# Transposed score pairs six slots behind the score pairs instead of five, and one DMA per half of the row maxima, in a fused ViT tower block

## The reference

```python
gray  = einsum('bchw,c->bhw', x, (0.2989, 0.587, 0.114))
edges = conv3x3(gray, scharr)                       # two filters
h     = (|edges[0]| + |edges[1]|) / 2               # 256 rows of 256: the tokens
h     = concat([cls_tok, h], axis=1)                # 257 tokens of width 256
y     = layernorm(h)
q, k, v = split(y @ w_qkv + b_qkv)                  # 16 heads of 16
att   = softmax(where(causal, q k^T / 4, -inf))     # 257 x 257, per head
h     = h + (att v) @ w_out + b_out
xq    = fake_quant(layernorm(h))                    # one scale for the whole tensor
u     = fake_quant(silu(xq @ wq_gate^T) * (xq @ wq_up^T))
out   = h + u @ wq_down^T
```

## Time and profile before

| | us |
|---|---|
| median of three runs | 1346.86 (1345.83 to 1353.33) |
| the profiled execution, its own time | 1357.62 |
| span of the profiled execution, first to last instruction | 1355.9 |
| PE busy, in the span | 1036.2 (76%) |
| DVE / ACT / POOL busy | 857.1 / 685.5 / 537.8 |
| mean granted TensorE clock | 0.881 of full speed |

### The profile page before, as it was taken

The page is one execution under the profiler, slowest core; times in us unless marked ns, Lnnn a source line. Parts: engine busy times, 40 slices in busy tenths (PEclk is TensorE's granted clock), DMA queues, the critical chain, the costliest instruction groups (busy, mean ns, idle before and its releaser), DMA issues. The chain is left out here.

```text
span 1355.9 us, 28643 instructions
## 1 busy us (share of the span) xinstructions
PE 1036.2 (76%) x9565; PEld 711.0 (52%) x9574; DVE 857.1 (63%) x1987; ACT 685.5 (51%) x1171; POOL 537.8 (40%) x645
## 2 busy tenths in 40 slices
PE   2458888888898988988898898887743766636665
PEld 1236666666666666666666666666532333313332
DVE  2134656667666676666676755664555888888664
ACT  1235555556555555655565555544223676633332
POOL 4244554465555555555555554543210000003222
PEclk9978989899999899999999988987766999976656
DMA  3565445555455554554565544423200334401764
GB/s 102 142 136 143 109 113 126 131 128 150 111 141 132 131 131 124 150 136 127 126 147 130 135 120 109 106 61 101 68 10 1 128 138 160 170 1 48 234 233 160
DMA packets 158498, 164.38 MB, mean 121 GB/s; under 512 B 29384, under 2 KB 153196, under 8 KB 155372
## 3 DMA queue, kind: packets, MB, share of 16 engines
q1 hardware_dynamic: 158444, 163.68, 44.4%
HBM read 73.26 MB, written 34.12 MB: 79 GB/s over the span
## 5 line engine op out<-in xcount | busy, mean ns | idle before, releaser
L519 ACT ACTIVATE prob<-ST 128x772 f32<-128x772 f32 x256 | 209.6, 819 | 218.3 <-PE ST L929 215.1
L684 DVE TENSOR_REDUCE mneg<-SX 128x2 f32<-128x258 f32 x256 | 107.6, 420 | 313.6 <-PE SX L915 313.1
L912 PE MATMUL SX<-kst,qst 96*128 96x257 bf16 (+1 forms) x1024 | 168.7, 259 | 44.1 <-DMA qst<-qpart 39.4
L929 PE MATMUL ST<-qst,kst 98*128 98x256 bf16 (+2 forms) x1536 | 145.5, 229 | 45.5 <-DMA qst<-mpart 45.0
L686 DVE TENSOR_REDUCE mneg<-SX 128x2 f32<-128x514 f32 x256 | 173.9, 679 | 0.0
L929 PEld LDWEIGHTS ST<-qst,kst 98*128 98x128 bf16 x1536 | 124.6, 102 | 69.3 <-DMA qst<-mpart 32.8
L915 PE MATMUL SX<-mask_s,ident_b 128*128 128x256 bf16 x512 | 148.2, 290 | 0.0
L912 PEld LDWEIGHTS SX<-kst,qst 96*128 96x128 bf16 x1024 | 97.1, 102 | 90.0 <-issue 64.3
L445 POOL TENSOR_SCALAR_AFFINE_SELECT prob<-prob 128x1016 f32<-128x1016 f32 x128 | 142.3, 1112 | 0.0
L1512 PE MATMUL GU<-qst,hq 128*128 128x256 bf16 (+1 forms) x384 | 87.2, 379 | 49.1 <-ACT hq L1303 49.1
L948 PE MATMUL G<-prob,vaug 128*32 128x256 f32 (+2 forms) x3072 | 118.9, 285 | 2.6 <-POOL prob L445 2.5
(11 more groups left out here) (228 smaller groups left out, 2106.0 us busy)
## 6 DMA issues: line engine op xcount, KB each, us to landing
kst<-kpart SPq DMA_DIRECT2D x192, 128.5 KB, 2.5
gst<-gray_dram SPq DMA_DIRECT2D x96, 256.0 KB
qst<-qpart SPq DMA_DIRECT2D x192, 128.0 KB, 2.4
h_dram<-hb SPq DMA_DIRECT2D x12, 1280.0 KB, 4.6
hb<-h_dram SPq DMA_DIRECT2D x12, 1280.0 KB, 6.1
wg_raw<-in_x SPq DMA_DIRECT2D x48, 256.0 KB, 4.0
wu_raw<-in_x SPq DMA_DIRECT2D x48, 256.0 KB, 4.1
gray_dram<-gray SPq DMA_DIRECT2D x64, 128.0 KB, 2.8
```

What stands on the lines that cost most here:

```text
L519: nc.scalar.activation(prob[:, g % 2, 2 * (u % 2):2 * (u % 2) + 2, 0:QEND], ST[:, :, 0:QEND], ACT.Exp).then_inc(exp_done, 1)
L684: nc.vector.tensor_reduce(mneg[:, 0, u // 4, 0, at], SX[:, :, S0:S0 + P + 1], AX.X, ALU.max, negate=True)
L912: mm(SX[:, r, at:at + k], qst[par][0:SR, 2 * u + r, P * t:P * t + P], kst[par][0:SR, 2 * u + r, 0:k], start=t == 1, stop=False)
L929: last = mm(ST[0:KEYS[k], r, QAT[k]:QAT[k] + QN[k]], kst[par_][:, i, KFIRST[k]:KFIRST[k] + KEYS[k]], qst[par_][:, i, Q0[k]:IMG], start=Tru ...
```

## The change

Four things are changed, all in the first stage.

1. The transposed pairs move one slot later: slot u now has `scores_t` of pair u+2 of `bT` (slots 0 to 5) and of pair u-6 of `bS` (slots 6 and 7); before, it was pair u+3 (slots 0 to 4) and pair u-5 (slots 5 to 7). ACT's exponentials move with them.
2. The PV quads move one slot later: quad 0 from slot 7 to slot 0 of the next step, quads 1, 2 and 3 from slots 1, 3 and 5 to slots 2, 4 and 6. POOL's `select` of quad 0 moves behind the two additions of the gray image.
3. `max_rows` sends both extra rows of a half (top and low part of the maxima) in one DMA instead of two.
4. DVE's `split(bS, 0)` is done before `edge_stats(bC)` instead of after it.

```diff
@@ sync: max_rows
                     wait(sp, msplit, b, 2, half_ + 1)
-                    for i in range(2):
-                        sp.dma_start(qst[par][SR + i:SR + i + 1, 8 * half_:8 * half_ + 8, :],
-                                     mpart[half_][8 * i:8 * i + 8, :]).then_inc(m_loaded[half_], 16)
+                    sp.dma_start(qst[par][SR:SR + 2, 8 * half_:8 * half_ + 8, :], mpart[half_][:, :]
+                                 ).then_inc(m_loaded[half_], 16)
@@ gpsimd: step
-                select(bS, 0)
                 if valid(bO):
...
                     nc.gpsimd.tensor_tensor(gray[:, :, :], gray[:, :, :], src(2), ALU.add).then_inc(gray_step, 1)
+                select(bS, 0)
@@ scalar: step
-                exponential(bT, 3)
+                exponential(bT, 2)
                 absolute(0)
                 keys(0)
+                exponential(bT, 3)
+                keys(1)
                 exponential(bT, 4)
-                keys(1)
-                exponential(bT, 5)
                 queries(0)
                 absolute(1)
-                exponential(bT, 6)
+                exponential(bT, 5)
...
                 unnormalised(0)
-                exponential(bT, 7)
+                exponential(bT, 6)
...
-                exponential(bS, 0)
+                exponential(bT, 7)
...
+                exponential(bS, 0)
                 unnormalised(1)
-                exponential(bS, 1)
...
-                exponential(bS, 2)
+                exponential(bS, 1)
@@ vector: step
                 edge_tile(bC, 1)
+                split(bS, 0)
                 edge_stats(bC)
-                split(bS, 0)
@@ tensor: step
                 scores(0)
-                scores_t(bT, odd, 3)
+                scores_t(bT, odd, 2)
                 edges(0)
                 keys(0)
+                outputs(bT, odd, 0)
                 scores(1)
+                scores_t(bT, odd, 3)
+                keys(1)
+                scores(2)
                 scores_t(bT, odd, 4)
                 outputs(bT, odd, 1)
-                keys(1)
-                scores(2)
-                scores_t(bT, odd, 5)
                 spread_rec()
                 queries(0)
                 edges(1)
                 scores(3)
-                scores_t(bT, odd, 6)
-                outputs(bT, odd, 2)
+                scores_t(bT, odd, 5)
                 queries(1)
                 turn_max(0)
                 scores(4)
-                scores_t(bT, odd, 7)
+                scores_t(bT, odd, 6)
+                outputs(bT, odd, 2)
...
                 project(0)
                 project(1)
                 scores(5)
+                scores_t(bT, odd, 7)
+                scores(6)
                 scores_t(bS, par, 0)
                 outputs(bT, odd, 3)
-                scores(6)
-                scores_t(bS, par, 1)
                 values()
                 transposes()
                 scores(7)
-                scores_t(bS, par, 2)
-                outputs(bS, par, 0)
+                scores_t(bS, par, 1)
                 turn_max(1)
```

More of the change, by code:

```diff
@@ L699, in split @@
                     wait(dve, mT_done, b, 2, half_ + 1)
-                    wait(dve, m_loaded[half_], b - 1, 32, 32)
+                    wait(dve, m_loaded[half_], b - 1, 16, 16)
                     nc.vector.tensor_copy(mpart[half_][:, :], M[1][0:H, 0:IMG]).then_inc(msplit, 1)
@@ L924, in scores_t @@
                         if u % 4 == 0:
-                            wait(pe, m_loaded[u // 4], b, 32, 32)
+                            wait(pe, m_loaded[u // 4], b, 16, 16)
                         for r in range(2):
```

## The result

| | before | changed |
|---|---|---|
| median of four runs, us | 1346.34 (1341.0 to 1353.33) | 1425.86 (1423.16 to 1429.68) |
| ratio, 95% interval | 1 | 1.0589 (1.0533 to 1.0646) |
| profiled execution, own time / span, us | 1357.62 / 1355.9 | 1423.16 / 1421.4 |
| mean granted clock in the span | 0.881 | 0.879 |
| mean step well inside the loop (19 periods of the keys' starts), us | 27.39 | 30.30 (28.7 to 32.2) |

The changed kernel is slower by 5.9%. The sum had 1423 us for the profiled execution, and that came to 1423.16. Against the median the forecast of 1412 is 14 us low: the profiled execution before lay 10.8 us over its median, the one after 2.7 under its own.

A forecast was written before the change was run, and what follows sets the result against it. A once-a-step chain through PE, DVE's copy and SP's DMAs bounds the kernel, 26.70 us; the late release adds 1.37 us and the slower clock 1.76, together 65 us: 1423 us profiled, 1412 us against the median, range 1376 to 1438.

The forecast's parts named there:

- The sum: Whole kernel: 54 us in 22 loop steps plus 11 us in eight others, 65 us over the profiled 1357.62 us.
- The chain and its link to SP: First-stage step: `scores(0)` to `turn_max(0)`, keys, next `scores(0)`; 13.40 + 5.01 + 9.66 = 28.07 us, against 26.70.
- the late release: kst is freed when old pair 7 ends, 4.98 us after `turn_max(0)`; SP's keys wait for it, 1.37 us more a step.
- the 1.23 us: SP's saving ahead of the keys: 0.72 from one DMA, up to 0.51 from the earlier copy; forecast to be waited away.
- The wait before `scores(6)`: PE waits about 0.8 us for DVE's maxima of pair 5 before `scores(6)`, where transposed pair 0 had stalled 1.18.
- The queries' last part: POOL finishes it 3.5 us after pair 7; SP wants it at 3.89, some 0.4 to spare; chance late 0.03.
- The clock: TensorE at half clock after longer waits before `scores(0)`: 1.76 us more from there to `turn_max(0)`, in 22 loop steps.
- no worse than now: Rival on TensorE's clock: only the 1.37 us a step in 30 steps, 41 us, giving 1388 us; chance 0.20.
- every step in the long form: Rival on TensorE's clock: every step starts slow, loop steps of 30.63 us, giving 1436 us; chance 0.15.
- The PV quads one slot later: PE's quads before and after `turn_max(0)`: no added cost; a late `select` of quad 0 taken as 0, bound 1.11 us.
- the 13.40: PE's work from `scores(0)` to `turn_max(0)` in us, forecast unchanged because two PV quads still lie in it.
- faster: Rival: kst's release is not late and the wait before `scores(0)` goes; 21 us less, 1326 us; chance 0.07.

The follow-up runs named there:

- e5: e3 plus one SP wait holding the keys' DMAs until the new image's transposed pair 0 is done; 1404.94 us, ratio 1.0432 to the kernel before.
- e9: Changed kernel with transposed pair 7 moved ahead of the projection, right behind PV quad 2; 1384.05 us, ratio 1.0229 to the kernel before.
- e1: Changed kernel with the maxima sent in two DMAs per half again; 1432.87 us, ratio 1.0593 to the kernel before.
- e4: Changed kernel with unused matmuls filling PE's waits, ten before and twelve behind `turn_max(1)`; 1380.98 us, ratio 1.0209 to the kernel before.
- e6: Kernel before with unused matmuls filling PE's waits, six before and five behind `turn_max(1)`; 1324.3 us, ratio 0.9873 to the kernel before.
- e3: Kernel before with only the single maxima DMA per half and the earlier copy (parts 3 and 4); 1296.69 us, ratio 0.9594 to the kernel before.
- e8: e3 with the PV quads one slot later and `select` of quad 0 behind the gray image; 1365.8 us, ratio 1.0162 to the kernel before.
- e11: e9 with `select` of quad 0 put back ahead of the gray image; 1502.21 us, ratio 1.1098 to the kernel before.
- e7: Kernel before with only the single maxima DMA per half (part 3); 1301.49 us, ratio 0.9682 to the kernel before.

## Why the prediction was right, point by point

- **The chain and its link to SP: right.** `turn_max(0)` to the keys 5.03 us (forecast 5.01), keys to the next start 9.70 (9.66), and the means of 16 steps are 5.02 and 9.68. e5, with the late release alone, and e9, with all but it, show that it acts. What was saved on SP was waited away: its queue stands still from 519.32 to 521.81 us, and e1 shows it for the DMA's 0.7 of the 1.23 us.
- **The wait before `scores(6)`: right.** 0.75 us (forecast 0.8), off the chain.
- **The queries' last part: right, and as near as forecast.** POOL ends it at 525.14 in the step shown, 0.6 us before SP wants it (forecast 0.4).
- **The clock: right in kind, slightly oversized.** 1.6 us a step by e4 against 1.76. Steps differ: the keys' starts lie 28.7 to 32.2 us apart, and 13 of 16 steps start slow. The kernel before had more slow starts (8 of 18) than the two rows let on, 0.7 us a step (e6). So neither "no worse than now" (28.07 us) nor "every step in the long form" (30.63 us) held, although the mean is nearer the latter. The rule of the Trainium skill (TensorE: Matmul & The Clock Gate, section "HAM oscillation — how this bites in real kernels"), by which each tile's wait sends the next one to the half clock, is borne out by 13 of the 16 steps, but not by every one.
- **"The PV quads one slot later ... Up to `turn_max(0)` PE has two of them as before, so the 13.40 stays ... If `select` of quad 0 ... is late ... I take 0": wrong.** The number of quads stayed, but not the time at which their inputs are ready, nor what quad 2 had covered by lying before `turn_max(0)`. It is 0.6 to 0.7 us a step on the chain (14.08 against 13.40 in e4), which I had left at nothing inside a bound of 1.11. Two of the waits stand in every step of the changed kernel too, 0.35 us before quad 1 and 0.31 before `turn_max(0)`; quad 0, the one I had thought of, waits only where a step starts at the full clock. The step came to 28.7 + 1.6 = 30.3 us against 28.07 + 1.76 = 29.83. In the sum this was nearly made up for: before, the loop's mean is 27.58 and not 27.37 us (its first periods, ahead of the stretch that I read, are longer), and outside the loop the loss was 7.9 and not 11, so that 66.5 us stand against 65. That the sum met the profiled execution within 1 us is luck: these misses cancel.
- **The price of the rival "faster": wrong.** It was the kernel without the late release, put at 21 us less than before. With the lag kept and pair 7 in time it is 31 us more (e9), since the quads and `scores(6)` then cost; with the single DMA and the earlier copy alone it is 55 less (e3). For the latter I had counted the wait before `scores(0)` and left out that with shorter waits the clock comes back (0.7 us a step by e6).

The costs don't add. Against e3, the late release alone costs 113 us (e5), the quads alone 76 (e8), and both 134. The changed kernel's step is only 0.7 us longer than e5's (30.30 against 29.59). I read this so: while SP holds the keys back, the quads' waits and that before `turn_max(1)` lie for the most part beside it, and so taking the late release out of the changed kernel gives 48 us (e9), not 113. The counterpart, the changed kernel with the quads alone put back, was not run.

Not tried: a third buffer for kst and qst, which would take the release away and leave the lag of six. Whether the lag would then pay for its quads stays open.

## What to carry to other kernels

When an operation is moved later, follow what it frees, not only what it feeds: the last reader of a buffer sets when the refill may be issued, and in an in-order queue everything behind the refill waits with it. Undo the parts of a mixed change one at a time before judging it: here two small parts were worth 55 us by themselves and were hidden under the other two, which cost 134. And a wait that was covered by a moved operation comes into view where that operation stood; look at both ends of the move.

## What the runs showed of the hardware

**DVE operations that take several times as long beside POOL.** By line in 300 to 800 us (count, busy us, mean ns of one, idle before), before:
```profile
L712 DVE TENSOR_TENSOR edge<-habs 128x256 f32<-128x256 f32 x36 | 23.0, 638 | 0.0
...
L726 DVE TENSOR_SCALAR ve<-ag 128x2 f32<-128x2 f32 x19 | 7.6, 400 | 0.7
```
and changed:
```profile
L711 DVE TENSOR_TENSOR edge<-habs 128x256 f32<-128x256 f32 x33 | 35.4, 1074 | 0.0
...
L725 DVE TENSOR_SCALAR ve<-ag 128x2 f32<-128x2 f32 x17 | 18.8, 1108 | 0.6
```
The operations are the same; what stands beside them has changed. Two runs differ in nothing but the place of POOL's `select`, e9:
```profile
L831 DVE TENSOR_SCALAR x<-h,ag,rstd 128x256 f32 x34 | 12.5, 410 | 0.0
```
and e11:
```profile
L831 DVE TENSOR_SCALAR x<-h,ag,rstd 128x256 f32 x30 | 38.5, 1322 | 11.8 <-POOL rstd L486 11.8
...
L692 DVE TENSOR_TENSOR mneg<-mneg,mtop 128x16 f32<-128x16 f32 x30 | 19.6, 655 | 1.0
```
L692 has 189 ns in e9. In the step shown of e11, L831 runs from 530.48 to 533.05 us while POOL adds up the gray image from 530.29 on, and L692, at 1.11 us, runs beside POOL's `select`. The Trainium skill (SBUF — State Buffer, section "Who interferes with whom") says that DVE and GpSimd share one pair of SBUF ports as an exclusive lock, which a DVE operation needs for a second SBUF input or in a mode that uses both ports, and that the later one waits for the whole of the other's instruction. These rows agree with it. Such an operation costs time only where something waits for it: e3, the faster kernel, has L725 at 1125 ns as well.

**One DMA of both maxima rows lands later than the second of two.** In e3 it takes from the end of the issue, 518.07 + 0.69 = 518.76, to the start of transposed pair 0, 521.74, that is 2.98 us; before it was 524.13 - 521.99 = 2.14 us. Over all such waits in 300 to 800 us the means are 2.88 and 2.07 us. But e7, in which the DMA is the only edit, has 2.52, so some 0.45 us go with the DMA's form and the rest with the other place of the copy. Still the one is better, since SP needs a single issue. The Trainium skill (DMA: Bandwidth & Descriptors, section "🔬 Why a DMA increments its semaphore by 16 and not by 1") has a DMA run on the largest number of engines up to 16 that divides the slowest dimension larger than 1 of both sides: 8 for each of the two, and 2 for the one. The direction agrees; which engines took part was not read off.

**Useless matmuls pay.** Filling the waits before a step's start gives back some 50 us (e4) and 17 us (e6), with the granted clock at 1.00 in 300 to 800 us in both.
